# First group's key and query rows from SBUF to SBUF in 24 DMAs, and an earlier first root and first scaling

## The reference, cut to what matters

```
q = layernorm(x) @ wq + bq          # 128 features = 16 heads of 8
k = ctx @ wk + bk ;  v = ctx @ wv + bv
attn = softmax(q k^T / sqrt(8)) ;  out = (attn v) @ wo + bo
x = x + tanh(g_xattn[0]) * out
```

## Time and profile before

| what | value |
|---|---|
| median of 3 runs | 818.73 us (818.16 to 818.75) |
| the profiled execution, time | 817.99 us |
| its span | 815.9 us |
| mean granted clock of PE | 0.908 |
| busy: PE, DVE, ACT, POOL | 674.6, 454.0, 396.9, 310.3 us |

### The profile page before, as it was taken

How to read it: one execution, slowest core, us unless ns; L and a number is a source line. 1 busy time by engine, 2 the same in 40 slices (tenths; PEclk the granted TensorE clock), 3 DMA queues, 4 the chain that set the end, 5 groups by cost and what they waited for, 6 DMA issues and landing times.

```text
span 815.9 us, 17391 instructions
## 1 busy us (share of the span) xinstructions
PE 674.6 (83%) x6461; PEld 566.0 (69%) x6461; DVE 454.0 (56%) x1407; ACT 396.9 (49%) x969; POOL 310.3 (38%) x266
## 2 busy tenths in 40 slices
PE   3698895499998997999989997884699848998873
PEld 3487782399898886787868644663699737877763
DVE  5376767432245576674757577336333426678672
ACT  4466450155464663665656574210355626665650
POOL 4564614435142373141322276004053284454121
PEclk9999996599999998999999999855599959999998
DMA  6542934757763010000000200004357543420000
GB/s 168 142 115 64 264 100 136 223 148 205 227 201 109 16 31 10 1 1 1 2 1 1 78 2 0 1 1 147 89 168 211 161 107 99 122 67 2 3 26 26
DMA packets 60716, 70.92 MB, mean 87 GB/s; under 512 B 7051, under 2 KB 40859, under 8 KB 60635
## 3 DMA queue, kind: packets, MB, share of 16 engines
q1 hardware_dynamic: 57563, 63.52, 27.3%
q0 software_dynamic: 3072, 6.30, 2.7%
HBM read 48.89 MB, written 20.91 MB: 86 GB/s over the span
## 4 chain that ended last, share of the span: by engine, by line
PE 66%; DVE 16%; issue 7%; ACT 5%; DMA 4%; SPq 1%; POOL 1%; POOLq 0%; DVEq 0%; ACTq 0%
PE banks L1402 8%; PE banks L1418 7%; PE banks L1514 4%; PE banks L1221 4%; PE banks L1534 3%; PE banks L1523 3%; PE banks L1244 3%; PE banks L1093 3%; PE banks L1135 3%; PE banks L1095 3%; PE banks L1094 3%; PE banks L1233 3%; PE banks L1567 2%; DMA xsb<-xs 2%; PE banks L1199 2%
## 5 line engine op out<-in xcount | busy, mean ns | idle before, releaser
L936 ACT ACTIVATE hT<-banks,wup 128x128 f32<-128x128 f32 x304 | 86.5, 368 | 74.4 <-PE banks L1402 64.0
L866 ACT ACTIVATE pT<-banks 77x512 f32<-77x512 f32 x128 | 69.0, 589 | 46.8 <-PE banks L1221 46.3
L586 POOL TENSOR_TENSOR kbd<-k,const 96x1248 fp32r<-96x1248 f32 x32 | 73.0, 2293 | 42.9 <-PE banks L1221 40.5
L679 POOL DMA_INDIRECT xs<-xn,slot x48 | 46.8, 974 | 108.9 <-DVE ysb L2160 52.7
L1402 PE MATMUL banks<-xTs,wup 128*128 128x128 f32 x608 | 84.9, 286 | 2.6 <-issue 1.4
L639 POOL TENSOR_TENSOR sh<-sh,rd 128x616 f32<-128x616 f32 x32 | 38.9, 1216 | 113.8 <-DVE rd L1805 113.2
L1418 PE MATMUL banks<-wd,hT 128*128 x608 | 80.8, 276 | 0.6 <-DVE ysb L2160 0.4
L1402 PEld LDWEIGHTS banks<-xTs,wup 128*128 128x128 f32 x608 | 78.5, 202 | 3.4 <-issue 3.2
L1418 PEld LDWEIGHTS banks<-wd,hT 128*128 128x128 f32 x608 | 73.8, 192 | 1.3 <-issue 1.1
L2160 DVE COPY ysb<-banks 128x128 f32<-128x128 f32 x76 | 22.1, 291 | 93.5 <-PE banks L1418 88.1
L566 POOL TENSOR_TENSOR rstd<-vv,const 128x4 f32<-128x4 f32 x24 | 24.5, 1020 | 114.3 <-DVE vv L1756 112.1
(11 more groups left out here) (317 smaller groups left out, 1590.2 us busy)
## 6 DMA issues: line engine op xcount, KB each, us to landing
wup<-in_up SPq DMA_DIRECT2D x76, 258.0 KB
q<-queries SPq DMA_DIRECT2D x24, 256.0 KB
queries<-qc SPq DMA_DIRECT2D x8, 512.0 KB
wd<-in_down SPq DMA_DIRECT2D x8, 512.0 KB
ys<-ysb SPq DMA_DIRECT2D x16, 256.0 KB
k<-keys SPq DMA_DIRECT2D x24, 156.0 KB, 3.5
xs<-zt SPq DMA_DIRECT2D x2, 1472.0 KB, 10.7
keys<-kc SPq DMA_DIRECT2D x8, 312.0 KB, 3.3
```

Source lines behind the costliest of these rows:

```text
L586: pool.tensor_tensor(kbd[b % NB8][0:96, :, :, :].bitcast(F32R), kb, m, ALU.mult).then_inc(h8.kbd, 1)
L679: pool.indirect_dma_start(xs[hh], bass.IndirectOffsetOnAxis(ap=idx[hh % 2][k_][:, t:t + 1], axis=0), xn8[hh % 2][:, t, :], None).then_inc( ...
L866: act.activation(pT[b % 2][0:SK, u, :], ps[0:SK, 2 + u % 2, :], ACT.Exp, scale=D8 ** -0.5)\
L936: ins = act.activation(hT[T % 3][:, c, :], ps[:, T % 2, c * P:c * P + P], func, bias=wup[T % NW][:, HID + c:HID + c + 1])
```

## The change

The first group's key and query rows no longer go through DRAM. A new function, first_roles, copies each 32-partition range of kc (and of qc) straight to its place in k (and q): 3 roles x 4 head groups = 12 DMAs for the keys, of 32 rows of 1248 bytes (39 KB), and 12 for the queries, of 32 rows of 2048 bytes (64 KB). Each adds 16 to kin or qin, so the thresholds on these semaphores change in all later waits, and those on kst and qst fall by one DMA. key_hi of group 2 now waits for the 12 key copies; key_hi of group 3 waits for the store of group 1, which is now the first store. Groups 1 to 3 of the first layer, and the last layer, keep the way through DRAM.

Besides, POOL's first root moves ahead of scratch8, ACT's scaled(0, 0) ahead of context(0), and PE's front(0) ahead of context(0).

```diff
@@ -373,20 +373,32 @@
 
                 sp.dma_start(k[1][96:P, :, :, :].rearrange("p u b t -> p (u b t)"), a["sel"]).then_inc(h8.pads, 16)
 
+            def first_roles(rows, split, cols, parts, lo, s_):
+
+                sp.wait_ge(lo, 1)
+                for part, r in parts:
+                    for u in range(4):
+                        sp.dma_start(rows[32 * r:32 * r + 32, u, :, :].rearrange("p b t -> p (b t)"),
+                                     f32(split[32 * u:32 * u + 32, part, 0:cols])).then_inc(s_, 16)
+
+            def roles_in(G):
+
+                return 16 * (12 + 3 * (G - 1))
+
             def store_keys(run, g):
 
                 G = g + NG * run
                 sp.wait_ge(h8.klo, G + 1)
-                if G:
-                    sp.wait_ge(h8.kst, 16 * G)
+                if G > 1:
+                    sp.wait_ge(h8.kst, 16 * (G - 1))
                 sp.dma_start(a["keys"][g].rearrange("p r n -> p (r n)"),
                              f32(kc[:, g % 2, :, :]).rearrange("p r n -> p (r n)")).then_inc(h8.kst, 16)
 
             def key_roles(run, g):
 
-                sp.wait_ge(h8.kst, 16 * (g + NG * run + 1))
+                sp.wait_ge(h8.kst, 16 * (g + NG * run))
                 if g:
-                    sp.wait_ge(h8.kin, 16 * 3 * (g + NG * run))
+                    sp.wait_ge(h8.kin, roles_in(g + NG * run))
                 if g >= 2:
                     sp.wait_ge(h8.kbd, 4 * (g + NG * run - 1))
                 for r, part in enumerate((0, 0, 1)):
@@ -397,8 +409,7 @@
 
                 G = g + NG * run
                 sp.wait_ge(h8.qlo, G + 1)
-                if G:
-                    sp.wait_ge(h8.qin, 16 * 3 * G)
+                sp.wait_ge(h8.qin, roles_in(G))
                 sp.dma_start(a["queries"], f32(qc[:, :, :])).then_inc(h8.qst, 16)
 
             def query_roles(run, g):
@@ -406,7 +417,7 @@
                 G = g + NG * run
                 if g >= 2:
                     sp.wait_ge(h8.st, 16 * (G - 1))
-                sp.wait_ge(h8.qst, 16 * (G + 1))
+                sp.wait_ge(h8.qst, 16 * G)
                 for r, part in enumerate((0, 1, 0)):
                     sp.dma_start(q[g % 2][32 * r:32 * r + 32, :, :, :].rearrange("p u b t -> p u (b t)"),
                                  a["queries"][:, part, :].rearrange("(u p) n -> p u n", u=4)).then_inc(h8.qin, 16)
@@ -466,7 +477,7 @@
                         load_slots(2 * run + 1, 4, nt, mo.xs1)
                     up_weights(j + NW)
                     if hh == 3 and i == 8:
-                        sp.wait_ge(h8.kin, 16 * 3 * NG)
+                        sp.wait_ge(h8.kin, roles_in(NG))
                         store_keys(1, 0)
                     if hh == 3 and i == 10:
                         key_roles(1, 0)
@@ -490,10 +501,8 @@
             sp.dma_start(tg[:, 0, :], row(a["g_xattn"]).to_broadcast([P, 4])).then_inc(ld.gate, 16)
             sp.dma_start(tg[:, 1, :], row(a["g_ffn"]).to_broadcast([P, 4])).then_inc(ld.gate, 16)
             sp.dma_start(x[:, GB:B, :], xd[:, GB:B, :]).then_inc(ld.xrest, 16)
-            store_keys(0, 0)
-            store_queries(0, 0)
-            key_roles(0, 0)
-            query_roles(0, 0)
+            first_roles(k[0], kc[:, 0, :, :], GB * SP, ((0, 0), (0, 1), (1, 2)), h8.klo, h8.kin)
+            first_roles(q[0], qc, GT, ((0, 0), (1, 1), (0, 2)), h8.qlo, h8.qin)
             store_keys(0, 1)
             key_roles(0, 1)
             store_keys(0, 2)
@@ -578,7 +587,7 @@
 
                 g, T = b // GB, b + B * run
                 if b % GB == 0:
-                    pool.wait_ge(h8.kin, 16 * 3 * (g + NG * run + 1))
+                    pool.wait_ge(h8.kin, 16 * (12 + 3 * (g + NG * run)))
                 if b >= NB8:
                     pool.wait_ge(h8.st, 4 * (T - NB8 + 1))
                 kb = k[g % 2][0:96, :, b % GB, :].unsqueeze(2).to_broadcast([96, HG, HG, SP])
@@ -652,9 +661,9 @@
             pool.memset(f32(chi[DC:K1, :, :]), 1.0)
             pool.memset(f32(clo[DC:K1, :, :]), 0.0).then_inc(su.zero, 1)
             pool.wait_ge(su.zero, 3)
-            scratch8()
             pool.wait_ge(ld.const, 16)
             rsqrt_front(0)
+            scratch8()
             rsqrt_front(1)
             keys(0, 0)
             keys(0, 1)
@@ -816,8 +825,10 @@
             def key_hi(run, g):
 
                 act.wait_ge(h8.kmm, g + NG * run + 1)
-                if g + NG * run >= 2:
-                    act.wait_ge(h8.kst, 16 * (g + NG * run - 1))
+                if g + NG * run == 2:
+                    act.wait_ge(h8.kin, 16 * 12)
+                if g + NG * run > 2:
+                    act.wait_ge(h8.kst, 16 * (g + NG * run - 2))
                 copy(kc[:, g % 2, 0, :], ps[:, 2 + g % 2, 0:GB * SP]).then_inc(h8.khi, 1)
 
             def pick_rows(run, first=0, last=NB8):
@@ -837,7 +848,7 @@
                     G = g + NG * run
                     act.wait_ge(h8.qmm, G + 1)
                     if G:
-                        act.wait_ge(h8.qin, 16 * 3 * G)
+                        act.wait_ge(h8.qin, 16 * (12 + 3 * (G - 1)))
                     act.activation(qc[:, 0, :], ps[:, 7, :], ACT.Identity, bias=bq).then_inc(h8.qhi, 1)
 
                 def own_values(g, bank):
@@ -1073,8 +1084,8 @@
                 copy(chi[0:DC, GB * g:GB * g + GB, 0:SK],
                      ps[0:DC, 3 + g, 0:GB * SP].rearrange("p (b t) -> p b t", b=GB)[:, :, 0:SK]).then_inc(su.hi, 1)
 
+            scaled(0, 0)
             context(0)
-            scaled(0, 0)
             front(0)
             heads8(0, 0)
             experts(0, ACT.Gelu)
@@ -1190,7 +1201,7 @@
 
                     T, q_ = T0 + b, q[b // GB % 2]
                     if pair == 0 and b % GB == 0:
-                        pe.wait_ge(h8.qin, 16 * 3 * (G0 + b // GB + 1))
+                        pe.wait_ge(h8.qin, 16 * (12 + 3 * (G0 + b // GB)))
                     if pair == 0:
                         pe.wait_ge(h8.kbd, T + 1)
                     if T or pair:
@@ -1709,8 +1720,8 @@
                                        const[0:SK, C_ID:C_ID + SK])
                 ins.then_inc(su.pe, 1)
 
+            front(0)
             context(0)
-            front(0)
             pe.wait_ge(su.zero, 3)
             heads8(0, 0)
             experts(0)
```

## The result

The changed kernel took 824.13 us, the median of 9 runs (821.43 to 827.89), against 817.05 for the kernel before in its 9 runs (810.32 to 819.48): a ratio of 1.0086 with a 95% interval of 1.0055 to 1.0117, some 7 us (4.5 to 9.6) slower. The forecast was 819.0, in a range of 817.1 to 821.7, with "no change" as the likeliest. One run of the kernel of experiment 9, 1130.68 us long at a granted clock of 0.556, is left out of its ratio.

A forecast was written before the change was run, and what follows sets the result against it. Bound: a line of dependent work, at the start through the store of keys 1. Terms -0.2 + 3.2 - 2.7 = +0.3 took the span from 815.9 to 816.2, with 2.09 around it 818.3, as a median 819.0; range 817.1 to 821.7.

The forecast's parts named there:

- What bounds the start: Chain to the first score matmul at 28.76 us: store of keys 1 lands at 27.50, then ACT and DVE work.
- A shift of the first score is a shift of the end: From the first score matmul on, the chain is unchanged, so its shift moves the end one for one.
- The issue of a copy, taken as 0.42 us: SP's 24 copy issues ahead of the store of keys 1: 24 x 0.42 = 10.1 us.
- The upper bound of 0.60: Highest price for one copy issue on SP, from the first k roles with their stall, 1.79 us for three.
- the two readings weighed there: SP's issue of 32 rows costs 0.48 us regardless, or depends on the DMA in front, giving 0.36 to 0.39.
- The stall of 0.4: SP's row of 24 issues: 0.4 us added for one stall of 0.95 us, half the time.
- The landing, 2.5: Store of keys 1 lands 2.5 us after issue instead of 5.20; bounds 2.2 and 3.4.
- ACT's new wait for them: ACT waits for the 12 key copies ahead of keys 2: costs 0 to 0.3 us, inside the wait for the store.
- The early root: POOL's root at about 6.75 us, scalings 8.1 to 9.75; keys 0 gain 0.2, queries' low part ends at 17.0.
- the clears are hidden: POOL's clears of vp and nm8 end near 11.9 us; their readers and POOL's next root come after 17.02.
- C: Rival: dear issues make SP the bound, 821.0 us at 0.48 an issue, 823.8 at 0.60; chance 0.24.
- D: Rival: small DMAs hold the DMA engines, store of keys 1 lands 10.4 us late, 829.1 us; chance 0.03.

The follow-up runs named there:

- experiment 9: Kernel before plus own halves for keys 2 and 3, the early root, scaling and transposes, and POOL's clears held until the weights are split: ratio 1.0009 (0.9977 to 1.0041).
- experiment 3: Kernel before with both stores kept and group 0's role DMAs cut into 24 pieces of 32 rows read from DRAM: ratio 1.0050 (1.0017 to 1.0084).

## Why the prediction was wrong

**What bounds the start: right.** Store of keys 1, ACT, DVE, first score: the same pieces, in the same order, in both chains.

**A shift of the first score is a shift of the end: right, as far as the times can tell.** By the ratios, times 817 us, five shifts of 3.9 to 6.1 us gave 4.1 to 7.9 us more time, and 8.4 gave 10.6. Each shift lies within its interval, but an interval is 2.5 to 3.6 us to either side, so "one for one" is not shown that sharply; and the three kernels whose first score is 1.3 to 1.9 us sooner show no gain, which the intervals allow too. One of the prediction's own signs of being wrong, a first score and an end that shift by different amounts, stands in the profiled pair (5.46 and 3.4): the step should have been kept apart from what one profile shows.

**The issue of a copy, taken as 0.42 us: this step failed.** It is 0.635. The term "24 x 0.42 = 10.1" measured 15.25, 5.2 us more, and that is nearly all of the missing shift: 15.29 + 15.25 + 2.44 = 33.0 for the landing, against 27.8 forecast. With measured terms the forecast's sum reads +0.30 (the start of the row) + 7.94 (its length) - 2.76 (the landing) = +5.48, where it had -0.2 + 3.2 - 2.7 = +0.3. The upper bound of 0.60 was below it too. Of the two readings weighed there the first came nearer: a DMA of 32 rows with DRAM on one side is 0.45 to 0.47 apart in series of its own kind. That would have been 1.1 us of the 5.2; the other 4.1 are what no row of before shows, that SBUF on both sides adds 0.17 an issue. The term stood on the middle of a wide range where the sign hung on it (no gain above 0.41), and that middle was used as if it were known.

**The stall of 0.4: wrong, none came.** Without it the forecast would have been further off by as much.

**The landing, 2.5: right** (2.44). Each key copy landed sooner after its issue than put (1.9 instead of 3.1), but the last was issued at 22.3, so they were in at 24.2 and not 22.5. ACT's new wait for them took 1.5 us instead of 0 to 0.3, inside the wait for the store, with no effect.

**The early root: half right.** The scaling ran from 8.23 to 9.88 (forecast 8.1 to 9.75) and the queries were split at 17.49 (17.0). But "the clears are hidden" was wrong: they held up DVE's cast until 12.0, and keys 0 came at 15.26 instead of 14.8, 0.5 us. The cover was checked for the readers of what the clears write, not for who works beside them. The Trainium skill, "SBUF — State Buffer", section "SBUF: two separate sides", has DVE (in some of its modes) and GpSimd share a port pair that one of them holds for a whole instruction, while the other waits. The casts that all end with the clears agree with a wait of that kind, but it was longer than one instruction: the cast at 9.12 sat out the rest of one clear of 1.81 us, the whole of the next and the short third. No run shows the mode of the cast, so the port stays an argument; that the clears are the cause is shown by experiment 9.

**The rivals.** C came about, an issue row in which SP is the bound, and with 0.635 it went beyond the dear end that it was given (0.60 an issue), though its 2.44 us of landing kept it near the 823.8 stated. That the median of 824.13 lies so near is partly luck: the forecast stands on 818.73, from three runs of the kernel before, and all nine give 817.05, so the measured loss is 7.1 us where that end of C has 5.1. C had 0.24, and the range stopped at 821.7 (C at 0.50 with a stall, which by its own terms is 821.5), since I read the ends of the issue price as unlikely when no row spoke for the middle. D (the DMA engines held by small copies) is out: they were busy 20% from 15.29 to 22.90, during the key copies, and 39% during the query copies. The Trainium skill, page "DMA: Bandwidth & Descriptors", section "Rules for kernel authors", is borne out in its advice to join small transfers (experiment 3), but for another reason here than the transfer's own overhead: the issuing queue. The same page says of the sequencer's time to start a DMA that it is "usually small relative to the DMA itself" (section "Issuing engines are not separate DMA queues"); here it is 0.59 us of SP for a DMA that lands in 2.0 us, and as the transfers overlap and the issues don't, the row of 24 is bound by the issues.

## What to carry to other kernels

Count DMA issues on the queue that releases the next stage, and price each from a row with the same two memories: a hop through DRAM that needs 8 issues and two landings can be shorter than 24 direct copies that need no landing between them. (Fewer direct copies, or a second queue to issue them, were not tried.) Where the sum changes sign inside the range of one unmeasured term, the forecast is that range and not its middle. When a clear or another filler is moved, look at what the neighbouring engine does in its new place, as well as at who reads the result.

## What the hardware showed that was not expected

- DMAs with SBUF on both sides are issued on SP 0.62 to 0.68 us apart, whatever their rows (8 to 128) and bytes (4 KB to 256 KB). With DRAM on one side it is 0.45 to 0.47 at 32 rows.
- A copy inside SBUF lands 1.9 (39 KB) or 2.0 to 2.1 us (64 KB) after its issue, and 24 in a row keep doing so.
- DVE's cast of 128 x 384 float32 took 0.36 us alone and up to 2.92 beside POOL's two clears of 2048 columns and a short one, always ending just after the last. DVE's subtraction for the low part of the keys, with one operand in PSUM, kept its 0.48 us beside the same clears (experiment 9, at 14.52).
- Nine runs of the kernel before spread from 810.3 to 819.5 us. The prediction took 0.2% for what can be told from no change; with 4 to 12 runs the intervals here are 0.3 to 0.45% on either side.
